# The sum over 16 gathered rows: four contiguous in-place additions in place of one strided reduction

## The chip, the core and the metric

The kernel runs on one core of a Trainium2 chip. The metric is the time of the whole program on the device, in microseconds: for the kernel before, the median of three runs is 8664.17 us (8647.6 to 8669.62).

## What is computed

The program is a small vision and language network in float32. An image tokenizer (four layers of a Fourier operator on 32 images of 64 x 64) makes 64 tokens for each image; with 128 text tokens they form 32 sequences of 192 tokens, 64 wide. Each passes a recurrence, a mixture of experts, an attention, and at the end a layer of product keys: for each token and each of 8 heads two top-16 searches give 256 candidate sums, of which the 16 best are kept. Their 16 indices point at rows of a table, their softmax gives 16 weights:

```
final_scores, pk_idx = jax.lax.top_k(score, FINAL_TOPK)
final_indices = jnp.take_along_axis(index, pk_idx, axis=-1)
final_scores = jax.nn.softmax(final_scores, axis=-1)
```

The keys row and the value row of an index, each 64 wide, are taken from the tables, weighted, and summed over the 16 indices of the token and head. The two sums (128 numbers) are a key and a value of a causal attention between the tokens, whose output is added to the input. The change lies in the weighted sum of the 16 rows. In the kernel the two tables stand side by side, so that one gathered row has 128 numbers.

## The kernel before

The 32 sequences are worked on in 16 pairs. A pair has 384 tokens, three tiles of 128 partitions. Each engine has a stream of instructions in an order fixed when the program is written: a helper (`weave`) merges several chains of sections by planned times (`STEPS`), the same way on all engines. A round does for one pair the front part (recurrence, experts, attention, keys), for the pair before it the row work and the back attention, and for the next group of images half of the tokenizer layers. A round has two windows: in the first the front chain runs beside a tokenizer layer and 11 row units, in the second the search (`v_top`), the back attention, another tokenizer layer and 13 row units. The first rounds have no row work, the last ones no tokenizer, and the very last only row work and the back attention.

A row unit is one tile of 128 tokens and one head: 24 for a pair, 384 in all. It goes through three engines:

- GpSimd (POOL), `pool_gather`, from L615: for each unit it waits for the indices (`kept_idx`, once for 8 units) and for a free buffer, and issues 16 indirect DMAs, one for each of the 16 indices (L624). Each takes a row of 128 numbers for each of 128 partitions. The buffer GATH has four slots (`RING = 4`), each 16 x 128 numbers in a partition.
- ScalarE (ACT), `a_consume`, from L834: it waits for the 16 gathers to land and multiplies each of the 16 rows by its weight, in place (L842).
- VectorE (DVE), `v_consume`, from L845: it waits for `multiplied` and sums the 16 rows into KV with one tensor_reduce over a rearranged view, in which the summed index is innermost and 128 elements apart (L849). Its completion raises `gather_free`, which allows POOL to fill this slot again four units later.

The indices come from `v_top` on DVE (from L769). For each of the three tiles it finds the top 16 of both halves, builds the candidate sums in a loop over the list CANDIDATES (tuples of four numbers, L794 to L797), searches again, subtracts the maximum and raises `shift_top` (L811). ACT takes the exponential (L976) and raises `exp_top`. DVE meanwhile looks the indices up with six groups of two tensor_tensor and one tensor_reduce (L818, L821, L824), writes IDX (L827), waits for `exp_top` of pair j and tile t, sums the exponentials (L829), makes the weights (L831) and raises `kept_idx`. In Python the loop over CANDIDATES uses the names i, n, j, m, and j is also the argument that holds the number of the pair: after the loop it is 0, the third number of the last tuple, `(8, 8, 0, 1)`. The wait `event("exp_top", j, t + 1)` stands behind that loop.

In what follows "drain" is the instruction that makes DVE wait for its own writes before the next instruction reads them.

Of the kernel before, what the change touches and what calls it, by code (L numbers as in the profile page):

```python
# [26 lines left out]
ALU = mybir.AluOpType  # L27
ACT = mybir.ActivationFunctionType
AX = mybir.AxisListType
# [21 lines left out]
def fourier_constants():  # L51
# [16 lines left out]
    for a in range(2):  # L68
# [12 lines left out]
H, TOPK, NK = 8, 16, 64  # L81


CANDIDATES = [(0, 1, 0, 8), (1, 1, 0, 4), (2, 1, 0, 2), (3, 1, 0, 2), (4, 4, 0, 1),
              (0, 1, 8, 8), (1, 1, 4, 4), (2, 1, 2, 3), (3, 1, 2, 2), (4, 1, 1, 2), (5, 3, 1, 1), (8, 8, 0, 1)]
# [8 lines left out]
RING = 4  # L94
# [99 lines left out]
def early_fusion(nc, xT, fc0, sw, cwb, fc1, fc2, f1, f2, g3, g4, txt, wrnn, brnn, gw, w1, w2, b2, wq, wk, wv, wot, wpk, keysT, wq5, wo5,  # L194
# [3 lines left out]
    with ctx:  # L198
# [49 lines left out]
        GATH = sb("GATH", [128, RING, TOPK, 2 * D]); KV = sb("KV", [128, NT3, H, 2 * D])  # L248
# [9 lines left out]
        S = {n: sem(n) for n in PER}  # L258
# [8 lines left out]
        def fence(e):  # L267

            e.sem_inc(passed[str(e.engine).split(".")[-1]], 1)


        def event(name, it, k):

            return S[name], (it + 1) * PER[name] + k
# [6 lines left out]
        def emptied(kind, it, name, k=0):  # L281

            b, n = number(PLANS[kind], name, k)
            return empt[kind, b], (it + 1) * total(PLANS[kind], b) + n + 1
# [484 lines left out]
        def v_top(e, j):  # L769
            for t in range(NT3):  # L770
                yield TOP_STEPS * t
                e.wait_ge(*emptied("front", j, "simA", t))
                fence(e)
                lists = [(p, h) for p in range(2) for h in range(H)]
                e.drain()
                for p, h in lists: e.max(V16[:, p, h, 0:8], SIM[:, t, p, 64 * h:64 * h + 64])
                e.drain()
                for p, h in lists:
                    if h == 0: yield TOP_STEPS * t + 1 + p
                    e.match_replace(SIMR[:, p, 64 * h:64 * h + 64], V16[:, p, h, 0:8], SIM[:, t, p, 64 * h:64 * h + 64], -FMAX)  # L780
                    e.max_index(I16[:, p, h, 0:8], V16[:, p, h, 0:8], SIM[:, t, p, 64 * h:64 * h + 64])
                yield TOP_STEPS * t + 3
                e.drain()
                for p, h in lists: e.max(V16[:, p, h, 8:16], SIMR[:, p, 64 * h:64 * h + 64])
                e.drain()
                for p, h in lists: e.max_index(I16[:, p, h, 8:16], V16[:, p, h, 8:16], SIMR[:, p, 64 * h:64 * h + 64])  # L786
                e.drain()
                yield TOP_STEPS * t + 4
                e.tensor_copy(IF[:, :, :, :].rearrange("p a h k -> p (a h k)"), I16[:, :, :, :].rearrange("p a h k -> p (a h k)")); e.drain()
                e.tensor_scalar(IF[:, 1, :, :], IF[:, 1, :, :], float(NK), None, ALU.mult); e.drain()  # L790
                e.tensor_tensor(IF[:, 1, :, :], IF[:, 1, :, :], HBASE[:, :].rearrange("p (h o) -> p h o", o=1).to_broadcast([128, H, TOPK]), ALU.add); e.drain()
                for src, dst in ((V16, C50), (IF, CI)):
                    at = 0
                    for i, n, j, m in CANDIDATES:  # L794

                        e.tensor_tensor(dst[:, :, at:at + n * m], src[:, 0, :, i:i + n].to_broadcast([128, H, m]) if n == 1 else src[:, 0, :, i:i + n],
                                        src[:, 1, :, j:j + m].to_broadcast([128, H, n]) if m == 1 and n > 1 else src[:, 1, :, j:j + m], ALU.add)  # L797
                        at += n * m
                yield TOP_STEPS * t + 5
                e.drain()  # L800
                for h in range(H): e.max(FV[:, h, 0:8], C50[:, h, :])
                e.drain()
                for h in range(H):
                    e.match_replace(CR[:, h, :], FV[:, h, 0:8], C50[:, h, :], -FMAX)
                    e.max_index(FP[:, h, 0:8], FV[:, h, 0:8], C50[:, h, :])
                e.drain()
                for h in range(H): e.max(FV[:, h, 8:16], CR[:, h, :])
                e.drain()
                for h in range(H): e.max_index(FP[:, h, 8:16], FV[:, h, 8:16], CR[:, h, :])

                e.tensor_tensor(FS[:, :, :], FV[:, :, :], FV[:, :, 0:1].to_broadcast([128, H, TOPK]), ALU.subtract); e.drain().then_inc(S["shift_top"], 1)  # L811
                yield TOP_STEPS * t + 5.5
                e.tensor_copy(PF[:, :, :], FP[:, :, :]); e.drain()
                for g, (h0, nh, k0, nc) in enumerate(LOOKUPS):
                    yield TOP_STEPS * t + 6 + g * 4 / len(LOOKUPS)
                    hit = EQ[:, 0:nh * 8 * nc].rearrange("p (h k c) -> p h k c", h=nh, k=8)
                    place = PF[:, h0:h0 + nh, k0:k0 + 8]
                    e.tensor_tensor(hit, IOTA[:, 0:nc].rearrange("p (a b c) -> p a b c", a=1, b=1).to_broadcast([128, nh, 8, nc]),  # L818
                                    place.rearrange("p h (k o) -> p h k o", o=1).to_broadcast([128, nh, 8, nc]), ALU.is_equal)
                    e.drain()  # L820
                    e.tensor_tensor(hit, hit, CI[:, h0:h0 + nh, 0:nc].rearrange("p h (o c) -> p h o c", o=1).to_broadcast([128, nh, 8, nc]), ALU.mult)  # L821
                    yield TOP_STEPS * t + 6 + (g + 0.6) * 4 / len(LOOKUPS)
                    e.drain()  # L823
                    e.tensor_reduce(place, hit, AX.X, ALU.add); e.drain()  # L824
                yield TOP_STEPS * t + 10

                e.tensor_copy(IDX[:, t, :, :], PF[:, :, :])  # L827
                e.wait_ge(*event("exp_top", j, t + 1))
                e.tensor_reduce(S8[:, 0, :], FS[:, :, :], AX.X, ALU.add); e.drain()  # L829
                e.reciprocal(S8[:, 1, :], S8[:, 0, :]); e.drain()  # L830
                e.tensor_tensor(WT[:, t, :, :], FS[:, :, :], S8[:, 1, :].rearrange("p (h o) -> p h o", o=1).to_broadcast([128, H, TOPK]), ALU.mult)  # L831
                e.drain().then_inc(S["kept_idx"], 1)
# [12 lines left out]
        def v_consume(e, i, u):  # L845

            yield u + 0.6
            e.wait_ge(*event("multiplied", i, u + 1))
            e.tensor_reduce(KV[:, u // H, u % H, :], GATH[:, u % RING, :, :].rearrange("p k d -> p d k"), AX.X, ALU.add).then_inc(S["gather_free"], 1)  # L849

        def v_keep_x(e, j, back, front):

# [465 lines left out]
        def VECTOR(e, k, i, j, g, l):  # L1318
            return {"forward0": lambda: v_forward(e, g, l, 0), "forward1": lambda: v_forward(e, g, l + 1, 0),
                    "inverse0": lambda: v_inverse(e, g, l, 0), "inverse1": lambda: v_inverse(e, g, l + 1, 0),  # L1320
                    "tokens": lambda: v_tokens(e, g), "rnn": lambda: v_rnn(e, j), "moe": lambda: v_moe(e, j), "att": lambda: v_att(e, j),
                    "pk": lambda: v_pk(e, j), "top": lambda: v_top(e, j), "back": lambda: v_back(e, k), "keep_x": lambda: v_keep_x(e, j, not isinstance(i, int) or i >= 0, not isinstance(i, int) or i < PAIRS - 1),
                    "rows": units(v_consume, e, i)}
# [114 lines left out]
```

## Time and profile before

| | |
|---|---|
| median of three plain runs | 8664.17 us |
| span of the profiled execution | 12469.6 us |
| PE busy | 6502.1 us (52%) |
| DVE busy | 5016.0 us (40%) |
| POOL busy | 5950.0 us (48%) |
| ACT busy | 3311.9 us (27%) |

The profiled execution has no time beside its span. It is much longer than a plain run: span and median are in the ratio 1.44. Busy times count execution alone, not waits or the sequencer's work. An idle time in the profile is put down to what ended it: an instruction on another engine, or "issue" where the profile shows nothing that the engine waited for.

### The profile page before, as it was taken

How to read it: one execution, taken by the hardware profiler on the slowest of the kernel's cores; microseconds unless marked ns; L12 is line 12 of the kernel's file. 1: busy time of each engine (PE TensorE's matmuls, PEld its weight loads, DVE VectorE, ACT ScalarE, POOL GpSimd, SP SyncE). 2: the span in 40 equal slices, each digit the busy share in tenths (PEclk: the TensorE clock that was granted, in tenths of full speed). 3: DMA queues.
4: the chain of work that ended last, by engine and by line, in shares of the span. 5: the costliest groups of instructions: out<-in, count | busy, mean ns of one | idle time of the engine just before them, and what ended most of it. 6: DMA issues, size and time to landing. Idle time of an engine off the chain costs nothing.

```text
span 12469.6 us, 153471 instructions
## 1 busy us (share of the span) xinstructions
PE 6502.1 (52%) x51536; PEld 4676.4 (38%) x51536; DVE 5016.0 (40%) x16213; ACT 3311.9 (27%) x9871; POOL 5950.0 (48%) x6157
## 2 busy tenths in 40 slices
PE   7845364555645566464654645555565555424203
PEld 6633243442534434343343433444344433213102
DVE  2253524435253443525345253452524435352612
ACT  2212222223222232222322222222322223222222
POOL 0024545445454554545455454454545445565573
PEclk7755555556555565555555555555555555555555
DMA  1011111111111111111111111111111111111110
GB/s 29 12 28 39 44 38 43 37 38 40 35 42 39 41 39 37 45 35 41 36 40 42 35 41 39 39 41 36 38 40 42 38 36 41 39 42 39 41 49 25
DMA packets 251313, 474.14 MB, mean 38 GB/s; under 512 B 130470, under 2 KB 130974, under 8 KB 250143
## 3 DMA queue, kind: packets, MB, share of 16 engines
q0 software_dynamic: 196608, 403.05, 12.2%
q1 hardware_dynamic: 53856, 60.52, 1.7%
q8 instruction: 442, 7.24, 0.2%
q14 instruction: 407, 3.33, 0.1%
HBM read 461.04 MB, written 2.10 MB: 37 GB/s over the span
## 4 chain that ended last, share of the span: by engine, by line
issue 30%; PE 29%; DVE 17%; another core or an unknown queue 16%; DVEq 5%; ACT 3%; DMA 0%; SPq 0%; ACTq 0%; POOL 0%; POOLq 0%
PE MM L417 3%; DVE KV L849 3%; PE PB L1107 3%; PE PB L1080 2%; ACT GATH L842 2%; PE PB L1145 2%; DVEq L823 2%; PE PB L1104 2%; PE PB L1121 2%; PE PB L1135 1%; PE MM L371 1%; DVE I L786 1%; DVE PF L824 1%; PE MM L432 1%
## 5 line engine op out<-in xcount | busy, mean ns | idle before, releaser
L624 POOL DMA_INDIRECT GATH<-in_table,IDX x6144 | 5946.4, 968 | 6393.3 <-DVE KV L849 3878.1
L842 ACT ACTIVATE GATH<-GATH,WT 128x128 f32<-128x128 f32 x6144 | 1902.5, 392 | 198.0 <-issue 197.1
L849 DVE TENSOR_REDUCE KV<-GATH 128x128 f32<-128x2048 f32 x384 | 1390.7, 3622 | 679.4 <-ACT GATH L842 407.6
L417 PE MATMUL MM<-SPEC,SW 32*32 32x8 f32 x25600 | 613.6, 196 | 1688.7 <-issue 1646.1
L417 PEld LDWEIGHTS MM<-SPEC,SW 32*32 32x32 f32 x25600 | 519.8, 147 | 1800.0 <-issue 1792.4
L485 ACT ACTIVATE U<-MM 128x320 f32<-128x320 f32 (+1 forms) x416 | 219.5, 528 | 1853.3 <-remote 879.6
L526 DVE COPY TURN<-TP 80x512 f32<-80x512 f32 (+1 forms) x512 | 347.2, 685 | 890.1 <-remote 440.0
L485 ACT ACTIVATE SPEC<-MM 128x160 f32<-128x160 f32 x320 | 96.1, 301 | 2238.0 <-PE MM L417 1423.5
L371 PE MATMUL MM<-F,TURN 128*128 128x80 f32 x2048 | 422.9, 375 | 442.0 <-DVE TURN L526 350.6
L371 PEld LDWEIGHTS MM<-F,TURN 128*128 128x128 f32 x2048 | 391.8, 284 | 506.0 <-issue 266.4
L456 PEld LDWEIGHTS MM<-G,TURN 80*128 80x128 f32 x2048 | 344.9, 241 | 522.7 <-issue 243.8
L456 PE MATMUL MM<-G,TURN 80*128 80x128 f32 x2048 | 362.5, 331 | 318.7 <-DVE TURN L526 149.3
L530 DVE COPY TURN<-TP 128x512 f32<-128x512 f32 (+1 forms) x320 | 217.6, 683 | 661.8 <-remote 262.7
L701 DVE COPY_PREDICATED Y<-OH,PB 128x192 f32<-128x192 int32 x128 | 47.4, 371 | 1054.8 <-PE PB L1107 765.5
L1107 PE MATMUL PB<-W2E,AREA 128*128 128x64 f32 x1536 | 419.0, 425 | 22.4 <-issue 22.4
L485 ACT ACTIVATE IMG<-MM,CONV 128x512 f32<-128x512 f32 x256 | 175.7, 686 | 959.1 <-PE MM L456 551.0
L1254 PE MATMUL PB<-AREA 128*64 128x64 f32 (+1 forms) x2304 | 319.6, 297 | 191.3 <-ACT AREA L1028 123.7
L432 PE MATMUL MM<-G,TURN 40*128 40x128 f32 x1280 | 320.7, 420 | 184.2 <-DVE TURN L530 121.7
L1080 PE MATMUL PB<-NTR,W1E 65*128 65x384 f32 x512 | 359.5, 854 | 31.6 <-ACT AREA L939 25.6
L1107 PEld LDWEIGHTS PB<-W2E,AREA 128*128 128x128 f32 x1536 | 348.2, 314 | 65.0 <-issue 21.4
L453 PE MATMUL MM<-IMG,CONV 128*128 128x512 f32 x512 | 348.9, 770 | 44.5 <-ACT IMG L485 29.2
L432 PEld LDWEIGHTS MM<-G,TURN 40*128 40x128 f32 x1280 | 273.7, 310 | 260.7 <-issue 212.9
(201 smaller groups left out, 11175.6 us busy)
## 6 DMA issues: line engine op xcount, KB each, us to landing
GATH<-in_table,IDX POOLq DMA_INDIRECT x6144
SW<-in_sw SPq DMA_DIRECT2D x160, 320.0 KB
CONV<-in_cwb SPq DMA_DIRECT2D x128, 4.0 KB
CONV<-in_cwb SPq DMA_DIRECT2D x128, 0.1 KB
U<-in_xT SPq DMA_DIRECT2D x16, 96.0 KB
out<-OUTB SPq DMA_DIRECT2D x16, 96.0 KB
W1E<-in_w SPq DMA_DIRECT2D x1, 520.0 KB
W2E<-in_w SPq DMA_DIRECT2D x1, 512.0 KB
```

The costliest lines, as they stand in the source:

```text
L371: m = e.matmul(p[:, 80 * j:80 * j + 80], TURN[:, c % 2, 128 * j:128 * j + 128], F1[:, :], start=True, stop=True)
L417: m = e.matmul(pv[r, :, k, :], SW[r, c % 2, k, :], Sv[r, :, c * MODES + k, :], start=True, stop=True)
L432: m = e.matmul(p[:, 128 * a:128 * a + 128], TURN[0:40, i % 2, 128 * a:128 * a + 128], G3[:, :], start=True, stop=True)
L453: e.matmul(p[:, :], CONV[:, 0:128], IMG[:, q, 512 * c:512 * c + 512], start=True, stop=False, skip_group_check=True)
L456: m = e.matmul(p[:, 128 * j:128 * j + 128], TURN[0:80, (CHUNKS + c) % 2, 128 * j:128 * j + 128], G4[:, :], start=False, stop=True, skip_gr ...
L485: e.activation(dst, MM[n % 2][src] if not callable(src) else src(MM[n % 2]), func, **kw).then_inc(mm_out, 1)
L526: e.tensor_copy(dst, TP[n % 2][0:rows, 0:cols]).then_inc(tp_out, 1)
L624: e.indirect_dma_start(GATH[:, r, k, :], None, table, bass.IndirectOffsetOnAxis(IDX[:, u // H, u % H, k:k + 1], 0)).then_inc(gath[r], 16)
L842: m = e.activation(GATH[:, r, k, :], GATH[:, r, k, :], ACT.Copy, scale=WT[:, u // H, u % H, k:k + 1])
L849: e.tensor_reduce(KV[:, u // H, u % H, :], GATH[:, u % RING, :, :].rearrange("p k d -> p d k"), AX.X, ALU.add).then_inc(S["gather_free"], 1)
L1080: e.matmul(PB[2 + n % 2][:, 0:TOK], W1[:, 128 * n:128 * n + 128], NTR[:, :], start=True, stop=True).then_inc(full["front", 2 + n % 2], 1)
L1107: m = e.matmul(o, HID[:, n % 4, 128 * t:128 * t + 128], W2[:, 64 * n:64 * n + 64], start=False, stop=(f == 1))
```

## The change

The one strided tensor_reduce becomes four tensor_tensor additions. The first adds rows 8 to 15 to rows 0 to 7 in place (1024 contiguous elements in a partition), the next two add the upper half of what is left to the lower (512, then 256), and the last adds row 1 to row 0 and writes KV (128). Each of the first three is followed by a drain. `gather_free` is raised by the last. The diff also renames the variables of the loop over CANDIDATES, so that j keeps the number of the pair.

```
-                    for i, n, j, m in CANDIDATES:
+                    for r0, n, r1, m in CANDIDATES:
 
-                        e.tensor_tensor(dst[:, :, at:at + n * m], src[:, 0, :, i:i + n].to_broadcast([128, H, m]) if n == 1 else src[:, 0, :, i:i + n],
-                                        src[:, 1, :, j:j + m].to_broadcast([128, H, n]) if m == 1 and n > 1 else src[:, 1, :, j:j + m], ALU.add)
+                        e.tensor_tensor(dst[:, :, at:at + n * m], src[:, 0, :, r0:r0 + n].to_broadcast([128, H, m]) if n == 1 else src[:, 0, :, r0:r0 + n],
+                                        src[:, 1, :, r1:r1 + m].to_broadcast([128, H, n]) if m == 1 and n > 1 else src[:, 1, :, r1:r1 + m], ALU.add)
...
             e.wait_ge(*event("multiplied", i, u + 1))
-            e.tensor_reduce(KV[:, u // H, u % H, :], GATH[:, u % RING, :, :].rearrange("p k d -> p d k"), AX.X, ALU.add).then_inc(S["gather_free"], 1)
+            rows = GATH[:, u % RING, :, :]
+            for n in (8, 4, 2):
+                e.tensor_tensor(rows[:, 0:n, :], rows[:, 0:n, :], rows[:, n:2 * n, :], ALU.add); e.drain()
+            e.tensor_tensor(KV[:, u // H, u % H, :], rows[:, 0, :], rows[:, 1, :], ALU.add).then_inc(S["gather_free"], 1)
```

## Rows read from the trace of the kernel before

**Rows 1.** The page: busy time by engine; lines of the chain; two costliest groups.

```profile
PE 6502.1 (52%) x51536; PEld 4676.4 (38%) x51536; DVE 5016.0 (40%) x16213; ACT 3311.9 (27%) x9871; POOL 5950.0 (48%) x6157
...
PE MM L417 3%; DVE KV L849 3%; PE PB L1107 3%; PE PB L1080 2%; ACT GATH L842 2%; PE PB L1145 2%; DVEq L823 2%; PE PB L1104 2%; PE PB L1121 2%; PE PB L1135 1%; PE MM L371 1%; DVE I L786 1%; DVE PF L824 1%; PE MM L432 1%
...
L624 POOL DMA_INDIRECT GATH<-in_table,IDX x6144 | 5946.4, 968 | 6393.3 <-DVE KV L849 3878.1
...
L849 DVE TENSOR_REDUCE KV<-GATH 128x128 f32<-128x2048 f32 x384 | 1390.7, 3622 | 679.4 <-ACT GATH L842 407.6
```

**Rows 2.** The waits: who waited for whom; us in total, times, longest.

```profile
POOL GATH L624 <- DVE KV L849: 3878.1, 296, 122.3
POOL GATH L624 <- issue: 2512.3, 5847, 661.2
```

**Rows 3.** Timeline of POOL, steady gathers: start us, length us, instruction, idle before.

```profile
7431.43 0.95 POOL L624 DMA_INDIRECT GATH<-in_table,IDX  x1 [0.30 <-issue]
7432.68 0.94 POOL L624 DMA_INDIRECT GATH<-in_table,IDX  x1 [0.30 <-issue]
```

**Rows 4.** Windows before the first gather and behind the last: busy by engine.

```profile
0.00:665.30 665.30, 536.90 (x6794) 408.49 (x6794) 187.97 (x556) 141.29 (x292) 3.59 (x13) 0.73 0.07 20
...
12343.80:12469.60 125.80, 86.50 (x496) 65.57 (x496) 39.13 (x68) 42.19 (x140) 0.02 (x1) 0.56 0.01 3
```

**Rows 5.** Timeline of ACT in the last stretch, row work alone.

```profile
11945.95 0.40 ACT L842 ACTIVATE GATH<-GATH,WT 128x128 f32<-128x128 f32 x1 [1.00 <-issue]
11947.35 0.40 ACT L842 ACTIVATE GATH<-GATH,WT 128x128 f32<-128x128 f32 x1 [1.00 <-issue]
```

**Rows 6.** Timeline of DVE: the reduction and the instruction behind it.

```profile
6188.83 3.62 DVE L849 TENSOR_REDUCE KV<-GATH 128x128 f32<-128x2048 f32 x1
6192.37 0.68 DVE L530 COPY TURN<-TP 128x512 f32<-128x512 f32 x1
```

**Rows 7.** Groups of DVE by shape: busy us, mean ns of one; idle before.

```profile
L821 DVE TENSOR_TENSOR SEARCH<-SEARCH 128x800 f32<-128x800 f32 x192 | 191.0, 995 | 14.7 <-issue 0.4
...
L821 DVE TENSOR_TENSOR SEARCH<-SEARCH 128x640 f32<-128x640 f32 x96 | 79.6, 829 | 9.0 <-issue 2.1
...
L909 DVE TENSOR_TENSOR AREA<-AREA,DEN 128x768 f32<-128x768 f32 x32 | 30.7, 958 | 2.4
...
L909 DVE TENSOR_TENSOR AREA<-AREA,DEN 128x512 f32<-128x512 f32 x32 | 22.3, 696 | 11.6 <-issue 9.7
...
L831 DVE TENSOR_TENSOR WT<-FS,S 128x128 f32<-128x128 f32 x48 | 14.6, 304 | 3.6
...
L909 DVE TENSOR_TENSOR AREA<-AREA,DEN 128x256 f32<-128x256 f32 x32 | 13.6, 426 | 8.2 <-issue 6.0
```

**Rows 8.** Timeline of all engines: gathers beside two-input instructions of DVE.

```profile
7400.99 1.02 DVE L818 TENSOR_TENSOR SEARCH<-IOTA,PF 128x800 f32<-128x800 f32 x1
...
7402.08 0.99 DVE L821 TENSOR_TENSOR SEARCH<-SEARCH 128x800 f32<-128x800 f32 x1
7402.24 1.66 POOL L624 DMA_INDIRECT GATH<-in_table,IDX  x1 [0.30 <-issue]
...
7404.20 0.95 POOL L624 DMA_INDIRECT GATH<-in_table,IDX  x1 [0.31 <-issue]
...
7404.46 0.96 DVE L909 TENSOR_TENSOR AREA<-AREA,DEN 128x768 f32<-128x768 f32 x1
```

**Rows 9.** Timeline of all engines: a gather beside the reduction.

```profile
9040.34 3.60 DVE L849 TENSOR_REDUCE KV<-GATH 128x128 f32<-128x2048 f32 x1
...
9041.54 0.94 POOL L624 DMA_INDIRECT GATH<-in_table,IDX  x1 [0.30 <-issue]
```

**Rows 10.** Line L624: length ns min/median/max, first and last start us.

```profile
L624 POOL DMA_INDIRECT GATH<-in_table,IDX x6144: 942/947/2362, 665.3 to 12342.9; - x199
```

**Rows 11.** Timeline of ACT: an exponential of the search.

```profile
762.91 0.31 ACT L976 ACTIVATE FS<-FS 128x128 f32<-128x128 f32 x1 [6.83 <-DVEq L811]
```

**Rows 12.** Timeline of DVE: the sum of the same exponentials.

```profile
782.79 0.28 DVE L829 TENSOR_REDUCE S<-FS 128x8 f32<-128x128 f32 x1
```

## The prediction, made before the changed kernel was run

> **What bounds the kernel now.** I read the page first, then the waits, then POOL, then the changed lines. The page [rows 1] shows no full engine: PE 52%, DVE 40%, POOL 48% of a span of 12469.6 us. The chain is spread over everything, and KV L849, the line of the change, holds 3% of it. That would make this a DVE question. But the profiled execution and the plain ones are far apart: 12469.6 us of span (no other time of it is shown) against a median of 8664.17 us, a factor of 0.695. So the question before any sum is what the 3805 us are, since the plain time is what is predicted.
>
> The waits [rows 2] answer it in part. POOL waited 3878.1 us for KV L849, and 2512.3 us for "issue". Of the latter, 661.2 us is the one wait before the first gather; 1851.1 us is left, in 5846 pieces, and the timeline [rows 3] shows what these are: a steady 0.30 us between gather instructions, so that one comes every 1.25 us whenever POOL isn't waiting for a buffer. A unit (16 gathers) thus takes 20.0 us of POOL. Cut the span at the first gather and the last [rows 4]: 665.3 us before, 125.8 us after. POOL with no wait for KV at all would need
>
> 665.3 + 5946.4 (busy) + 1851.1 (the small gaps) + 125.8 = 8588.6 us.
>
> The plain median is 75.6 us above that, 0.9%. My reading: in the profiled execution the other engines are held back, POOL waits for them, and without the profiler those waits are all but gone. The engine holding back can be seen in the last stretch, where ACT has only row work [rows 5]: multiplications of 0.40 us come at steps of 1.40 us with "issue" before them; nothing of the program released them late. In the same trace POOL's own step does not vary. So I take the plain execution as bound by POOL's gather instructions, with at most some 76 us of other waits, although the profiled one is not. This is the choice on which all hangs; it is inferred from a sum that fits, not seen.
>
> **What the change removes.** 384 strided reductions of 3.622 us [rows 1]. The next DVE instruction starts 0.08 us before the end (6188.83 to 6192.37 [rows 6]), so a step is 3.54 us.
>
> **What it adds.** 384 times four tensor_tensor of 1024, 512, 256 and 128 elements. Nearest rows [rows 7]: 800 elements 0.995, 640 elements 0.829, 768 elements 0.958, 512 elements 0.696, 256 elements 0.426; the 128-wide WT line is 0.304 us. From 640 to 800 an element costs 1.04 ns, so 1024 cost 0.995 + 224 x 1.04 ns = 1.228 us. Sum 1.228 + 0.696 + 0.426 + 0.304 = 2.654. After a drain the next starts 0.07 to 0.08 us late (L818 at 7400.99 for 1.02, L821 at 7402.08 [rows 8]): three of these, 0.22, less the overlap of 0.08 at the end: a step of 2.79 us. Saving on DVE: 0.75 us x 384 = 288 us at most, and nothing at worst if the strided step also hurt the new form, which contiguous rows exclude. The Trainium skill ("VectorE: DVE Perf Modes", the perf-mode tier table) gives tensor_reduce one element per cycle and about 2.29 us for 2048 fp32 elements in tensor_tensor at the same rate; by that the change would lengthen the step by half a microsecond. The trace shows 3.62 us for this strided reduction, and that decides; the tensor_tensor rows agree with the page's rate.
>
> **What of the saving lies on the path.** In the profiled execution: 3% of 12469.6 is 374 us, or some 103 of the 384 reductions on the chain; 103 x 0.75 = 77 us. In the plain one, if POOL is full, none of it: POOL is not waiting for KV, and DVE waits for gathers. An earlier KV frees a ring buffer earlier, and POOL has free buffers already.
>
> **What the new form does to POOL.** A two-input DVE instruction stops POOL's gather. At 7402.08 L821 (both inputs in SBUF) runs 0.99 us; the gather that began at 7402.24 takes 1.66 instead of 0.95 us and ends 0.83 us after L821 [rows 8]. Beside the reduction L849 (9040.34 to 9043.94) the gather at 9041.54 takes 0.94 us [rows 9], and one that has begun before the two-input instruction (7404.20, with the two-input L909 from 7404.46) takes 0.95 us [rows 8]. So a gather is held when it starts while such an instruction is running, until that one ends plus 0.82 us, against 0.95 us from its own start: the delay is the rest of the running instruction less 0.13 us. With a start every 1.25 us, at a random place, an instruction of length L costs POOL (L - 0.13)² / (2 x 1.25) on average: for 1.228 us 0.48 us. If that one held a gather, the next starts 1.12 us after its end, inside the third addition's last moments (about 0.02 us); so the 0.696, 0.426 and 0.304 us additions cost little more. I take 0.50 us for each unit while POOL runs. Bounds: nothing (the gather always starts outside) and 1.10 us (it always starts with the addition). A second way to the same number: gathers take 968 ns in the mean and 947 in the median [rows 1, 10], so the trace holds 6144 x 0.021 = 129 us of such delays, under some 640 us of long two-input instructions (L821 191.0 + 79.6 us, L818 ahead of each as long, L909 30.7 + 22.3 + 13.6, L732 as wide and as many as the first of these [rows 7]), 0.20 us for each us. The additions are 384 x 2.654 = 1019 us: 206 us, and more where POOL runs all the time.
>
> The Trainium skill ("SBUF — State Buffer", who interferes with whom) says that tensor_reduce never contends with GpSimd, with which the 0.94 us agrees, and that a DVE instruction with two SBUF inputs contends with a GpSimd one that reads SBUF. It adds, as inferred, that tensor_tensor does not stall descriptor generation; the 1.66 us rows differ, so the trace decides. By that inference POOL would keep its pace and the time would stay at 8664.
>
> DVE itself pays some 0.03 us in an instruction that a gather starts beside (L818 at 7400.99: 1.02 instead of 0.99 us [rows 8]), which stays off the path.
>
> **The renamed loop variables.** In the kernel before, the loop over the candidates left j at 0, so the wait for exp_top before L829 asked for pair 0's count, which from the second pair on is long reached. Now it asks for the true pair: 48 real waits instead of 3. In the trace the tightest case is ACT's exponential ending at 763.22 and DVE's L829 at 782.79 [rows 11, 12], 19.6 us later: between them stand six lookups, each of two two-input instructions and a reduction. The wait costs nothing while ACT is that early. Queued behind it are WT, kept_idx and so the next pair's gathers.
>
> **Sum.** POOL adds 384 x 0.50 = 192 us. Of the 76 us of waits left I let 10 absorb (they are spread over 384 units; a delay within a unit isn't caught by a wait elsewhere). 8664 + 182 = 8846 us, 2.1% slower.
>
> **Rivals.**
> - *POOL is full and held (forecast).* 8846 us; its own range 8740 to 8960 (0.2 to 0.78 us a unit). Chance 0.62.
> - *POOL has slack in plain executions too.* For it: the profile shows POOL waiting for KV before 296 of 384 units [rows 2], and the 0.30 us gap may be partly the profiler's. Then the DVE saving counts: 77 us by the chain, 8587; all of it 288 us, 8376. It decides once the waits left in the plain execution exceed the 192 us added: 76 + 384 x (20.0 - u) > 192, a unit u below 19.7 us. Chance 0.22.
> - *Both at once.* Half of the units in stretches where POOL is full (+0.50), half where it waits for KV or DVE leads (-0.5 on average): within 26 us of 8664. Also here: the additions don't hold gathers. Chance 0.13.
> - *The restored wait bites.* In the last stretch of the profile ACT needs 16 x 1.40 = 22.4 us for 16 multiplications [rows 5]; if one such unit stood between shift_top and the exponential, each of 48 waits would cost a few us, 48 x 3 = 144 us: 8808. Against it: 19.6 us at the least. Chance 0.03, the same side as the forecast.
>
> Change and no change are told apart at 0.3%, 26 us. Slower 0.64, within 0.13, faster 0.23. The range of 8 in 10 reaches into the second rival: 8570 to 8940.
>
> **What would show it.** In the profile after: four additions of about 1.23, 0.70, 0.43 and 0.30 us where L849 stood, step 2.8 us; DVE busy down by some 370 us (384 x 0.97). Gathers beside the first addition at up to 2.0 us, the mean of L624 up from 968 to 975 ns or more, POOL's wait for KV down. The profiled span, where POOL waits, may well fall by some 50 to 100 us while the plain time rises: that split is the mark of my reading. Wrong would be a plain time below 8640: then POOL is not full, or not held. If the mean of L624 doesn't move, the hold is not there. A stop of DVE before L829 would show the restored wait.

## The result and the profile after

The changed kernel takes 8862.5 us (median of 4 runs, 8829.66 to 8872.15), the kernel before, run beside it and earlier, 8656.11 us (4 runs): the ratio is 1.0237, 95% interval 1.0214 to 1.0261. It is 206 us slower.

The profiled execution after has a span of 8870.3 us, as long as a plain run. The profiled one before, 12469.6 us [rows 1], is not its partner. The kernel runs in two kinds of executions, about 8650 us and about 12500 us, plain runs as well as profiled ones. Each set of runs in the experiments was made on a chip of its own and showed one kind only (two sets the first, three the second). I call them short and long. Runs are compared within a kind. The partner in the short kind is the profile of rename_only_2, the strided reduction with the renamed loop (8633.45 us). First its page, then that of the changed kernel; the columns are those of [rows 1].

```profile
PE 5931.8 (69%) x51536; PEld 4347.3 (50%) x51536; DVE 4965.8 (57%) x16213; ACT 3285.6 (38%) x9871; POOL 5952.8 (69%) x6157
...
POOL 57%; issue 20%; PE 16%; DVE 4%; DVEq 1%; ACT 1%; DMA 0%; POOLq 0%; SPq 0%; ACTq 0%
...
L624 POOL DMA_INDIRECT GATH<-in_table,IDX x6144 | 5949.2, 968 | 2592.3 <-issue 2527.7
```

```profile
PE 5953.9 (67%) x51536; PEld 4363.1 (49%) x51536; DVE 4591.7 (52%) x17365; ACT 3281.1 (37%) x9871; POOL 6160.7 (69%) x6157
...
POOL 68%; issue 22%; PE 7%; DVE 2%; DVEq 0%; ACT 0%; POOLq 0%; SPq 0%; DMA 0%; ACTq 0%
...
L624 POOL DMA_INDIRECT GATH<-in_table,IDX x6144 | 6157.2, 1002 | 2613.4 <-issue 2553.0
```

DVE got 374 us less work and the kernel became slower. POOL's gathers are 68% of the chain, after 57%. Nearly all of POOL's idle time is "issue", time in which it waited for no other engine; rename_only_2, then the changed kernel:

```profile
POOL GATH L624 <- issue: 2527.7, 6127, 659.7
ACT GATH L842 <- DMA GATH<-in_table,IDX: 1849.7, 203, 16.1
```

```profile
POOL GATH L624 <- issue: 2553.0, 6140, 681.8
ACT GATH L842 <- DMA GATH<-in_table,IDX: 2392.5, 250, 16.6
```

ACT waits 2392.5 us for gathered rows (1849.7 us with the strided reduction), where in the long execution before it was POOL that waited, 3878.1 us for DVE [rows 2]. Line L624 gives POOL's remaining wait and the first and last gather; again rename_only_2, then the changed kernel:

```profile
L624 POOL DMA_INDIRECT GATH<-in_table,IDX x6144: 942/947/2362, 663.8 to 8544.8; - x199
its engine sat idle before it (us, times) until:
  issue: 2527.7, 6127
  DVE KV L849: 64.7, 17
```

```profile
L624 POOL DMA_INDIRECT GATH<-in_table,IDX x6144: 939/947/2540, 685.9 to 8773.8; - x199
its engine sat idle before it (us, times) until:
  issue: 2553.0, 6140
  DVE KV L852: 60.5, 4
```

With these the two spans can be written as POOL's time (the gaps are "issue" less its longest, which is the wait before the first gather):

| us | strided | changed | difference |
|---|---|---|---|
| before the first gather | 663.8 | 685.9 | +22 |
| gathers, busy | 5949.2 | 6157.2 | +208 |
| gaps of 0.30 us | 1868.0 | 1871.2 | +3 |
| waits for KV | 64.7 | 60.5 | -4 |
| behind the last gather | 97.2 | 95.5 | -2 |
| span | 8642.9 | 8870.3 | +227 |

The loss is in the length of the gathers: 208 / 384 = 0.54 us a unit. The 22 us of the first row are no part of it: the first gather starts at 663.8 us in rename_only_2 and at 682.0 us in rename_only, which is the same kernel. One unit of the changed kernel in the timeline:

```profile
7014.87 2.48 DVE L851 TENSOR_TENSOR GATH<-GATH 128x1024 f32<-128x1024 f32 x3
7015.33 1.58 POOL L624 DMA_INDIRECT GATH<-in_table,IDX  x1 [0.30 <-issue]
...
7017.21 0.96 POOL L624 DMA_INDIRECT GATH<-in_table,IDX  x1 [0.30 <-issue]
...
7017.43 0.29 DVE L852 TENSOR_TENSOR KV<-GATH 128x128 f32<-128x128 f32 x1
7017.63 0.68 DVE L767 COPY AREA<-PB 128x512 f32<-128x512 f32 x1
```

The first addition runs from 7014.87 to about 7016.09 (its mean length is 1.222 us); the gather that starts within it takes 1.58 us and ends 0.82 us behind it, much as at [rows 8]. The next one starts at 7017.21, in the third addition's last moments, and loses 0.01 us.

One unit is an example; the whole trace can be counted: sort the gathers by the DVE instruction that is running when they start, and sum what they take beyond the median gather (947 ns). In the changed kernel 383 gathers start in a first addition, about one for each unit, and take 185 us more. Of the 299 that start more than 0.15 us before that addition's end, 283 end 0.80 to 0.83 us behind it; the other 16 are not held. Another 376 start in a third addition, 5 us more. In rename_only_2 1071 gathers start in a strided reduction, and together they take 0.1 us more. So 190 of the 208 us lie in gathers that start inside the new instructions.

The four additions by shape:

```profile
L851 DVE TENSOR_TENSOR GATH<-GATH 128x1024 f32<-128x1024 f32 x384 | 469.3, 1222 | 969.3 <-ACT GATH L842 963.2 <-issue 1.5
L851 DVE TENSOR_TENSOR GATH<-GATH 128x512 f32<-128x512 f32 x384 | 265.9, 692 | 28.6
...
L851 DVE TENSOR_TENSOR GATH<-GATH 128x256 f32<-128x256 f32 x384 | 163.4, 426 | 30.7 <-issue 2.6
L852 DVE TENSOR_TENSOR KV<-GATH 128x128 f32<-128x128 f32 x384 | 112.3, 293 | 31.9 <-issue 3.5
```

### The profile page after: what moved, and what is told of

It reads as the page before. It is cut to its first block, busy times and chain, and to the rows that moved or that the text cites. A ratio compares the mean times of both kernels' runs of the same rounds, so it can differ in the third digit from the quotient of the medians.

```text
span 8870.3 us, 155845 instructions
## 1 busy us (share of the span) xinstructions
PE 5953.9 (67%) x51536; PEld 4363.1 (49%) x51536; DVE 4591.7 (52%) x17365; ACT 3281.1 (37%) x9871; POOL 6160.7 (69%) x6157
## 4 chain that ended last, share of the span: by engine, by line
POOL 68%; issue 22%; PE 7%; DVE 2%; DVEq 0%; ACT 0%; POOLq 0%; SPq 0%; DMA 0%; ACTq 0%
POOL GATH L624 68%; PE MM L417 1%; PE MM L371 1%; PE PB L1110 1%; PE MM L432 1%; PE PB L1083 0%; PE MM L453 0%; PE MM L394 0%; PE MM L456 0%; PE PB L1107 0%; PE TP L365 0%; PE TP L426 0%; PE MM L352 0%; PE PB L1257 0%; PE TP L449 0%
## 5 line engine op out<-in xcount | busy, mean ns | idle before, releaser
L624 POOL DMA_INDIRECT GATH<-in_table,IDX x6144 | 6157.2, 1002 | 2613.4 <-issue 2553.0
L842 ACT ACTIVATE GATH<-GATH,WT 128x128 f32<-128x128 f32 x6144 | 1885.0, 390 | 2392.8 <-DMA GATH<-in_table,IDX 2392.5
L851 DVE TENSOR_TENSOR GATH<-GATH 128x1024 f32<-128x1024 f32 (+2 forms) x1152 | 898.7, 780 | 1028.5 <-ACT GATH L842 963.2
L526 DVE COPY TURN<-TP 80x512 f32<-80x512 f32 (+1 forms) x512 | 345.3, 683 | 497.6 <-PE TP L449 284.9
L417 PE MATMUL MM<-SPEC,SW 32*32 32x8 f32 x25600 | 409.0, 197 | 238.0 <-issue 141.3
L1257 PEld LDWEIGHTS PB<-AREA 128*64 128x64 f32 (+1 forms) x2304 | 255.3, 191 | 620.1 <-issue 570.7
L417 PEld LDWEIGHTS MM<-SPEC,SW 32*32 32x32 f32 x25600 | 385.8, 148 | 278.4 <-issue 267.3
L371 PE MATMUL MM<-F,TURN 128*128 128x80 f32 x2048 | 374.3, 344 | 138.0 <-DVE TURN L526 133.3
L371 PEld LDWEIGHTS MM<-F,TURN 128*128 128x128 f32 x2048 | 349.3, 257 | 183.0 <-issue 130.7
L456 PEld LDWEIGHTS MM<-G,TURN 80*128 80x128 f32 x2048 | 316.1, 223 | 218.3 <-issue 130.2
L530 DVE COPY TURN<-TP 128x512 f32<-128x512 f32 (+1 forms) x320 | 217.4, 682 | 356.0 <-PE TP L388 206.2
L456 PE MATMUL MM<-G,TURN 80*128 80x128 f32 x2048 | 320.6, 307 | 42.7 <-DVE TURN L526 42.6
L1218 PE MATMUL PB<-NT,W 64*64 64x384 f32 x256 | 137.7, 673 | 289.5 <-ACT AREA L989 279.6
```

Source lines behind the costliest of these rows:

```text
L371: m = e.matmul(p[:, 80 * j:80 * j + 80], TURN[:, c % 2, 128 * j:128 * j + 128], F1[:, :], start=True, stop=True)
L417: m = e.matmul(pv[r, :, k, :], SW[r, c % 2, k, :], Sv[r, :, c * MODES + k, :], start=True, stop=True)
L456: m = e.matmul(p[:, 128 * j:128 * j + 128], TURN[0:80, (CHUNKS + c) % 2, 128 * j:128 * j + 128], G4[:, :], start=False, stop=True, skip_gr ...
L526: e.tensor_copy(dst, TP[n % 2][0:rows, 0:cols]).then_inc(tp_out, 1)
L624: e.indirect_dma_start(GATH[:, r, k, :], None, table, bass.IndirectOffsetOnAxis(IDX[:, u // H, u % H, k:k + 1], 0)).then_inc(gath[r], 16)
L842: m = e.activation(GATH[:, r, k, :], GATH[:, r, k, :], ACT.Copy, scale=WT[:, u // H, u % H, k:k + 1])
```

## The experiments

Theory "hold": POOL is full, and a gather that starts beside a two-input DVE instruction is held. Its rivals are the restored wait, and DVE's work, drains or count of instructions. The first nine runs fell in the long kind. There the theory can be tested for the hold itself, but not for its effect on the time; the times that the expectations give for the short kind are not tested by them.

**Only the rename (long kind).** The strided reduction kept, the loop's names changed (also in the two lines below it, left out here):

```
-                    for i, n, j, m in CANDIDATES:
+                    for r0, n, r1, m in CANDIDATES:
...
```

> The strided reduction of the kernel before, with the renamed loop variables alone, so that the wait for the exponentials is a real one for all 48 tiles. Theory 'hold' (the additions stop POOL's gathers, POOL is full): the wait plays no part, 8656 us within 0.3%, mean of L624 well below the 1002 ns of the changed kernel, some 965 to 980 ns, and POOL's wait for KV small. Rival 'wait' (the restored wait makes the time): 8800 us or more, with DVE idle before L829. It also gives a profile of the strided reduction in an execution that is as long as a plain one.

12479.6 us against 12470.97: ratio 1.0, interval 0.9988 to 1.0011. In the short kind (rename_only_2, below) 0.999. The restored wait costs nothing; that rival is out. The mean of L624 was 968 ns as expected, but POOL's wait for KV was 3893.6 us and not small. The run also showed that plain runs of the kernel before take 12471 us on this chip, so a span of 12469.6 us needs no profiler to explain it.

**Only the additions (long kind).** The loop keeps its old names:

```
-            e.tensor_reduce(KV[:, u // H, u % H, :], GATH[:, u % RING, :, :].rearrange("p k d -> p d k"), AX.X, ALU.add).then_inc(S["gather_free"], 1)
+            rows = GATH[:, u % RING, :, :]
+            for n in (8, 4, 2):
+                e.tensor_tensor(rows[:, 0:n, :], rows[:, 0:n, :], rows[:, n:2 * n, :], ALU.add); e.drain()
+            e.tensor_tensor(KV[:, u // H, u % H, :], rows[:, 0, :], rows[:, 1, :], ALU.add).then_inc(S["gather_free"], 1)
```

> The four additions alone, with the loop variables as before (the wait for the exponentials passes without waiting from the second pair on). Theory 'hold': as the changed kernel, 8862 us within 0.3%. Rival 'wait': back at 8656 us.

12354.85 us: ratio 0.9908, interval 0.9892 to 0.9924, 116 us *faster*. Neither of the times that I expected came, and the sign is the finding: the additions gain where POOL waits for KV and lose where POOL is full. The gathers are held here too, but POOL waits less; rename_only, then adds_only:

```profile
L624 POOL DMA_INDIRECT GATH<-in_table,IDX x6144 | 5947.2, 968 | 6421.6 <-DVE KV L849 3893.6
```

```profile
L624 POOL DMA_INDIRECT GATH<-in_table,IDX x6144 | 6003.3, 977 | 6211.2 <-DVE KV L852 3674.6
```

The gathers take 56 us more, and POOL waits 219 us less for KV.

**The reduction twice (long kind).**

```
+            e.tensor_reduce(KV[:, u // H, u % H, :], GATH[:, u % RING, :, :].rearrange("p k d -> p d k"), AX.X, ALU.add)
+            e.drain()
             e.tensor_reduce(KV[:, u // H, u % H, :], GATH[:, u % RING, :, :].rearrange("p k d -> p d k"), AX.X, ALU.add).then_inc(S["gather_free"], 1)
```

> The strided reduction done twice for each unit, with a drain between, so that DVE has 384 x 3.6 = 1390 us more work and each buffer comes free 3.6 us later, by an instruction with one input. Theory 'hold': POOL is not stopped by it and has free buffers, so 8656 us within 1%. Rival 'DVE' (the changed kernel is slower because of what DVE does or how late it frees the buffer, by drains or by more instructions): clearly slower, several hundred us, since this adds more DVE time than the change ever could.

13221.79 us, ratio 1.0593 (1.0573 to 1.0613): 751 us for 1369 us more of DVE. In this kind somewhat over half of DVE's added work shows in the time.

**One gather less (long kind).**

```
-                for k in range(TOPK):
+                for k in range(TOPK - 1):
                     e.indirect_dma_start(...)
...
-            e.wait_ge(gath[r], (i * (NT3 * H // RING) + u // RING + 1) * 16 * TOPK)
+            e.wait_ge(gath[r], (i * (NT3 * H // RING) + u // RING + 1) * 16 * (TOPK - 1))
...
+                e.memset(GATH[:, :, TOPK - 1, :], 0.0)
```

> One of the 16 gathers of each unit is left out (the last row is a row of zeros; ACT and DVE work on 16 rows as before). Theory 'hold', its first half (POOL is full): 384 x 1.28 us = 490 us less, 8160 to 8200 us. Rival 'POOL has slack': under 100 us less.

11965.91 us, ratio 0.9592 (0.9577 to 0.9607): 505 us less, 1.32 us for each gather left out. The saving is the one that a full POOL would give (490 us expected), although POOL still waited 3933.1 us for KV: each gather costs at least its full step of 1.25 us even where POOL has slack. Saving and waits together fitted neither picture and led to the runs with 28 gathers below.

**A wide addition for nothing, and the additions in narrow pieces (long kind).** The first keeps the reduction and adds one addition behind it:

```
-            e.tensor_reduce(KV[:, u // H, u % H, :], GATH[:, u % RING, :, :].rearrange("p k d -> p d k"), AX.X, ALU.add).then_inc(S["gather_free"], 1)
+            e.tensor_reduce(KV[:, u // H, u % H, :], GATH[:, u % RING, :, :].rearrange("p k d -> p d k"), AX.X, ALU.add)
+            rows = GATH[:, u % RING, :, :]
+            e.drain()
+            e.tensor_tensor(rows[:, 0:8, :], rows[:, 0:8, :], rows[:, 8:16, :], ALU.add).then_inc(S["gather_free"], 1)
```

> The strided reduction is kept and makes the result; behind it one in-place addition 1024 wide is run on the same rows for nothing, and it frees the buffer. DVE has 1.3 us more work for each unit than before, in one two-input instruction. Where the kernel before takes 8656 us (POOL full), theory 'hold': 384 x 0.48 = 184 us more, 8840 us, almost as much as the whole change, mean of L624 about 30 ns above that of a kernel with the reduction alone. Rival 'drains and count' (it is the number of instructions and drains that costs): a quarter of the change's loss, 8700 us. Where the kernel before takes 12471 us (POOL waiting), both expect 0.54 of the DVE time added, from the double reduction's 751 us for 1390: some 270 us more, 12740.

12820.11 us against 12639.4: ratio 1.0148 (1.0122 to 1.0175), 181 us, less than the 270 expected. The second makes the changed kernel's sum in 15 additions, each 128 wide:

```
             for n in (8, 4, 2):
-                e.tensor_tensor(rows[:, 0:n, :], rows[:, 0:n, :], rows[:, n:2 * n, :], ALU.add); e.drain()
+                w = min(n, 1)
+                for k in range(0, n, w):
+                    e.tensor_tensor(rows[:, k:k + w, :], rows[:, k:k + w, :], rows[:, n + k:n + k + w, :], ALU.add)
+                    e.drain()
```

> The changed kernel's sum in 15 additions, each 128 wide (0.293 us), with a drain behind each: the same elements, no strided reduction, more instructions, DVE busy 4.4 us for a unit instead of 2.65. Where POOL is full, theory 'hold' with the delay of a gather as (L - 0.13)^2 / 2.5 for an instruction of length L: 15 x 0.011 = 0.16 us for a unit, 61 us, 8717 us, mean of L624 20 ns or more below the changed kernel's. Rival 'hold by total time' (0.20 us for each us of two-input work, whatever its pieces): 384 x 4.4 x 0.20 = 338 us, 8990 us. Rival 'drains and count': slower than the changed kernel as well. Where POOL waits (12471 us before): DVE's extra 2 us for a unit count, some 12800 to 12900 us.

12999.31 us, ratio 1.0277 (1.0251 to 1.0303), 360 us. The times tell little here; the length of the gathers does. Reduction and wide addition, then the narrow pieces:

```profile
L624 POOL DMA_INDIRECT GATH<-in_table,IDX x6144 | 5975.8, 973 | 6692.3 <-DVE GATH L852 4179.7
```

```profile
L624 POOL DMA_INDIRECT GATH<-in_table,IDX x6144 | 5953.1, 969 | 6928.4 <-DVE KV L855 4392.7
```

Against the strided kernel's 5947.2 us: one wide addition +29 us, four of falling width +56 us, fifteen of 0.29 us +6 us, though these are 1684 us of two-input work and the four 1011. These differences carry an error: the undisturbed gather is not quite equally long in all runs (the median is 944 ns with the one wide addition, 947 ns in the others, and 3 ns of 6144 gathers are 18 us). Counted as above, each against its own median:

| long kind | gathers that start in an added instruction | us more | each |
|---|---|---|---|
| one wide addition | 119 | 50 | 0.42 |
| four additions, the first | 109 | 64 | 0.59 |
| fifteen narrow additions | 305 | 13 | 0.04 |

A gather that starts at a random place in an instruction of length L loses (L - 0.13)² / 2L by the prediction's rule: 0.49 us for 1.22 us, 0.05 us for 0.29 us. So the hold goes with the length of the piece, and "0.20 us for each us" is refuted as a rule. In the long kind only 109 gathers start in a first addition, against 383 in the short one, since POOL often waits just then.

**28 gathers a unit (long kind).** Both sums, with 12 more gathers of 32 numbers into a buffer that nothing reads (ACT waits for these too):

```
+                for k in range(12):
+                    e.indirect_dma_start(MORE[:, r, k, :], None, table.rearrange("r (q d) -> (r q) d", q=4), bass.IndirectOffsetOnAxis(IDX[:, u // H, u % H, k:k + 1], 0)).then_inc(gath[r], 16)
```

> The strided reduction with the renamed loop, and 12 more gathers for each unit, of 32 numbers a partition into a buffer that nothing reads: 28 gathers instead of 16, so that POOL needs 35.0 us for a unit, more than the 32.5 us that a unit takes where the kernel before runs 12471 us. It makes POOL full whatever the other engines do: 665 + 384 x 28 x 1.25 + 126 = 14230 us and the holds of the search's instructions, some 200 us, so 14400 to 14500 us, with POOL's wait for KV nearly gone. It is the partner of the next run.

> The same with the four additions: where POOL is full, theory 'hold' wants them slower than their partner by 384 x 0.50 = 192 us (1.3%), mean of L624 and its fellow line up by 18 ns (192 us over 10752 gathers). Rival 'the loss belongs to the faster executions and has nothing to do with POOL being full': not slower than the partner, rather 50 to 120 us faster, as adds_only was against 12471 us.

18748.47 us strided, 18583.96 us with the additions, where 14400 was expected: POOL did not get full, it waited 4325.1 and 4131.0 us for KV. The additions are 164.5 us faster than their partner, as adds_only was, and their L624 is held as there (5997.7 us after 5940.6). This pair therefore says nothing of the loss with a full POOL.

12 x 384 gathers cost 6088 us, 1.32 us each, the same price as the one left out. In the long kind the other engines are slowed while POOL gathers. Counted over rename_only, PE starts 2.2 matmuls for each us in which POOL runs and 6.9 in which it waits, and is busy for 42% and 67%; DVE is busy for 35% and 53%. In rename_only_2 PE starts 5.6 for each us in which POOL runs. Two neighbouring windows of rename_only show an extreme case, PE's line L417 alone (columns: stretch, length, PE busy and count, PEld busy and count, clock, DMA share, GB/s); in the first POOL ran 17 gathers, in the second it stood still:

```profile
7795.50:7815.50 20.00, 1.34 (x8) 0.98 (x8) 0.50 0.20 53
7816.00:7836.00 20.00, 7.46 (x420) 6.65 (x419) 0.50 0.08 22
```

There are 8 matmuls against 420. In the changed kernel's short execution the same line makes 480 in 20 us beside 16 gathers:

```profile
5062.00:5082.00 20.00, 7.76 (x480) 7.33 (x480) 0.50 0.30 82
```

The granted clock is 0.50 in all three, 1.2 GHz, so it isn't the clock. This is what I had laid to the profiler: in the long kind the others fall behind while POOL runs, and POOL then waits until they have caught up. What makes an execution long is open. Every set had its own chip and its own time, so the runs don't even tell whether it goes by chip.

**The search's instructions in pieces (long kind, then short).**

```
+                    kk = 4 if nc > 20 else 8
+                    for h in range(nh):
+                        for k in range(0, 8, kk):
+                            e.tensor_tensor(hit[:, h, k:k + kk, :], ..., ALU.is_equal)
+                            e.drain()
```

and the same for the multiplication.

> The strided reduction with the renamed loop, and the search's two-input instructions L818 and L821 (800 or 640 wide) in pieces of 200 or 160, a drain between any two: DVE has some 0.66 us x 576 = 380 us more, a gather is held 0.09 instead of 0.30 us by each. Where POOL is full (8656 us before), theory 'hold' expects 576 x 0.21 = 122 us less, 8534 us: a version that beats both kernels. Where POOL waits (12471 us), DVE counts: 0.54 x 380 = 200 us more. Mean of L624 in either case 10 to 20 ns below that of the strided kernel.

12846.26 us, ratio 1.0146 (1.0125 to 1.0167), 186 us more where 200 was expected; the mean of L624 is 954 ns, within what was expected.

**Short kind: the reduction twice.**

> The strided reduction done twice, as in reduce_twice, for an execution in which the kernel before takes about 8656 us; all experiments so far fell where it takes 12471 to 12660 us and POOL waits. Where POOL is full, theory 'hold': within 1% of 8656 us, no more POOL wait for KV than some 100 us, mean of L624 some 35 ns below the changed kernel's 1002. Rival 'DVE': several hundred us more. Where it takes 12500 us: 750 us more, as measured.

9248.96 us against 8659.65: ratio 1.0692 (1.0658 to 1.0726), 589 us. My expectation (within 1%, at most some 100 us of wait) failed, and the rival's number came. The page and the line tell which way it went:

```profile
DVE 33%; PE 32%; DVEq 12%; issue 10%; POOL 10%; ACT 2%; DMA 0%; SPq 0%; POOLq 0%; ACTq 0%
...
L624 POOL DMA_INDIRECT GATH<-in_table,IDX x6144 | 5944.4, 968 | 3203.5 <-issue 2528.6
```

The gathers are as short as ever and POOL waits 674.9 us for KV: with the doubling DVE and PE lead the chain, 33% and 32%. So DVE's slack in the short kind is less than these 1368 us. The loss of this kernel and that of the changed one are different losses: here POOL waits and isn't held, there it is held, doesn't wait, and DVE has less work than before.

**Short kind: the partner profile, and the pieces.**

> The strided reduction with the renamed loop variables again, for a profile where the kernel before takes about 8656 us: the partner that the changed kernel's profile lacks. Theory 'hold': 8656 us within 0.3%; POOL's wait for KV under 150 us against 60.5 in the changed kernel's profile, mean of L624 968 to 975 ns against 1002, so that the hold (6144 x 27 to 34 ns = 166 to 209 us) makes the 206 us of the change; POOL the largest share of the chain. Rival 'DVE or the wait': POOL's rows the same in both. Where the kernel before takes 12500 us: as measured, no difference.

8633.45 us against 8645.02 (0.999, 0.9979 to 1.0002), POOL 57% of the chain, a wait of 64.7 us and a mean of 968 ns: what "hold" expected. It is the left column of the table above.

> The strided reduction with the search's wide two-input instructions in pieces, for an execution in which the kernel before takes about 8656 us. DVE gets some 300 us more work. In the slow executions the mean of L624 fell from 968 to 954 ns. Theory 'hold': with POOL full 6144 x 14 ns = 86 us less or somewhat more, 8530 to 8590 us, faster than both kernels although DVE does more. Rival 'DVE' (DVE's work or its drains set the time, as in reduce_twice_3, where 1386 us more gave 589): slower, some 8750 us. Where the kernel before takes 12500 us: 1.5% slower, as measured.

8698.74 us, ratio 1.0049 (1.0031 to 1.0067), slower by 54 us where 55 to 115 less was expected.

```profile
PE 35%; DVE 27%; POOL 18%; issue 11%; DVEq 5%; ACT 2%; DMA 0%; SPq 0%; POOLq 0%; ACTq 0%
...
L624 POOL DMA_INDIRECT GATH<-in_table,IDX x6144 | 5854.4, 953 | 2768.2 <-issue 2541.5
```

L624 became 94.8 us shorter than in rename_only_2, about as expected; some 18 us of that are the median gather again (944 ns after 947), the rest is hold. But POOL's wait for KV rose from 64.7 to 226.7 us: with 269 us more of DVE work, PE and DVE lead the chain. Neither POOL nor DVE has much slack, and 95 us saved on one are lost with the work put on the other. So this run shows that the pieces shorten the gathers, and not that shorter gathers make the kernel faster. No version here beats the strided reduction in the short kind.

## Why the prediction was right

- *The plain kernel is bound by POOL's gathers.* Right for the executions that were predicted: chain 68%, wait for KV 60.5 us. The sum of 8588.6 us left 76 us of waits; the partner profile shows 64.7.
- *The profiler holds the other engines back.* Wrong. Plain runs take 12471 us too, on another chip. The sum fitted because the long kind adds its time to POOL's waits and leaves POOL's own step at 1.25 us. The result was right and the reason was not: that was luck.
- *The step of DVE, 2.79 us.* Measured 2.76 (7014.87 to 7017.63); the first addition 1.222 against 1.228, DVE busy 374 us less against 372.
- *0.50 us a unit of hold, 192 us.* Measured 0.54 us and 208 us. The law gave 0.48 us for the first addition; counted, it is 185 us, 0.48 us a unit. The second way, 0.20 us for each us of two-input work, gave 206 us by accident.
- *A gather that has begun before the two-input instruction is not held.* Mostly right. In the changed kernel 453 gathers start outside any tensor_tensor and have one of over 0.65 us starting less than 0.95 us behind them; 36 of them take 1.72 to 2.54 us all the same; these 36 start while L526, L530, L561 or L723 is running just ahead of it. The gathers of this sort that are held cost 41 us, against 19 us in rename_only_2, which is about the rest of the 208 us. Why they are held is not shown.
- *10 us absorbed.* POOL's waits fell by 4.
- *77 us of saving by the chain where POOL has slack* (the rival): measured 116 us in the long kind. The rival was true, of other executions. Its price was too low: the chain names what ended last, while the doubled reduction cost 0.55 us for each us of DVE work there.
- *The restored wait costs nothing.* Right, 1.0 and 0.999.
- *What I missed:* how little slack DVE has beside a full POOL. It was called off the path, but 1368 us more of it cost 589 us and 269 us more cost 54.

The causal claim rests on three things: the table of the two short executions, in which little but the gathers' length moves; the count, which finds 190 of the 208 us in gathers that start inside the additions; and the runs with wide, narrow and no additions, whose gathers lengthen as the law says. A kernel that keeps the additions and loses the hold in the short kind was not run.

## What to carry to other kernels

Before counting a saving on one engine, write the plain time as the sum of another engine's busy time, gaps and waits: an engine that is left with hardly any wait is the bound, even at 69% busy. Then ask what the new form does to that engine: here 374 us of DVE work were saved and 208 us of POOL's time were spent, because a reduction has one input and an addition two. And if profile and plain times disagree, get a profile of the same length before trusting either's waits.

## What the runs showed of the hardware

- A gather instruction of POOL that starts while a DVE instruction with two SBUF inputs runs ends 0.82 us behind it, but never before its own 0.94 us are over: 283 of 299 did in the changed kernel. The 1071 that start in a strided reduction take 0.1 us more together. In the long kind fifteen additions of 0.29 us with drains, 1684 us of work, cost the gathers that started in them 13 us, the first of four, 1.22 us long, 64 us. The Trainium skill ("SBUF — State Buffer", who interferes with whom) says that such an instruction contends with a GpSimd one that reads SBUF, and the runs agree; that tensor_tensor leaves descriptor generation alone, its inference, they don't bear out.
- A strided reduction costs 3.62 us for 2048 elements, four contiguous additions of 1920 elements together 2.63 us. It is the stride that costs: the contiguous reductions of L824 take 0.986 us for 800 elements and 0.820 us for 640, from which I estimate 2.3 us for 2048. A contiguous reduction of this sum was not run.
- One program has two speeds, 8650 and 12500 us; each of five sets of runs, on five chips, showed one of them, and the cause is open. In the slow one PE starts 2.2 matmuls for each us in which POOL gathers and 6.9 in which it waits; in one pair of windows it was 8 and 420 in 20 us, at the same granted clock of 0.50. Each gather costs 1.32 us of the whole there.
